# One transformer layer on one core: the first chunk's front of the last stage placed beside attention's last group

## The reference, cut to what matters

```python
x   = L0_attn_x                                   # (4, 1024, 128), 16 heads of 8
S   = Q @ K^T / sqrt(8), causal;  attn = softmax(S);  O = attn @ V
x1  = layernorm(x + O @ W_o.T + b_o)
sim = (x1 @ Wq) against keys                      # 2 x 4 heads x 64 keys per token
sx, sy = top 8 of each half;  scores = top 8 of sx[i] + sy[j]      # per head
w   = silu(x1 . down_embed[idx]) * softmax(scores)
y   = silu(x1 @ Wg + bg) * (x1 @ Wu + bu) @ Wd + bd + sum_k w_k * up_embed[idx_k]
out = layernorm(x1 + y)
```

## Time and profile before

| | us |
|---|---|
| median of 3 runs (840.32 to 843.26) | 842.15 |
| the profiled execution | 842.8 |
| its span on the core | 841.1 |
| TensorE busy | 731.9 (87%) |
| Vector busy | 683.3 (81%) |
| ScalarE busy | 567.9 (68%) |
| GpSimd busy | 423.4 (50%) |
| granted TensorE clock, mean | 0.941 of full |

### The profile page before, as it was taken

How to read it: one execution, slowest core, us unless ns; L and a number is a source line. 1 busy time by engine, 2 the same in 40 slices (tenths; PEclk the granted TensorE clock), 3 DMA queues, 4 the chain that set the end, 5 groups by cost and what they waited for, 6 DMA issues and landing times. The chain is left out here.

```text
span 841.1 us, 17303 instructions
## 1 busy us (share of the span) xinstructions
PE 731.9 (87%) x4345; PEld 328.1 (39%) x4345; DVE 683.3 (81%) x2289; ACT 567.9 (68%) x926; POOL 423.4 (50%) x468
## 2 busy tenths in 40 slices
PE   6768999999999999999999998677888798888755
PEld 4422333333333333333333332333556456555345
DVE  5979998998998989989989971066888888888883
ACT  4710466766676766667757678368879788897771
POOL 8880121122112211322132212368999999999984
PEclk9965799999999999999999999698999999999997
DMA  7984435533653454436433331201010101100000
GB/s 195 278 219 93 98 94 120 126 86 82 130 125 74 91 131 115 87 80 140 115 81 85 84 84 35 76 4 50 1 38 1 39 0 39 39 1 13 14 1 26
DMA packets 58954, 67.05 MB, mean 80 GB/s; under 512 B 15488, under 2 KB 33536, under 8 KB 58880
## 3 DMA queue, kind: packets, MB, share of 16 engines
q1 hardware_dynamic: 53120, 62.35, 31.2%
q10 hardware_dynamic: 5184, 2.36, 1.0%
q0 software_dynamic: 576, 1.57, 0.6%
HBM read 46.73 MB, written 19.53 MB: 79 GB/s over the span
## 5 line engine op out<-in xcount | busy, mean ns | idle before, releaser
L699 ACT ACTIVATE probs<-ps 128x384 f32<-128x384 f32 (+2 forms) x384 | 291.5, 809 | 175.1 <-PE ps L753 172.9
L670 POOL TENSOR_SCALAR_AFFINE_SELECT probs<-probs 128x256 f32<-128x256 f32 x256 | 102.8, 406 | 363.3 <-ACT probs L699 360.7
L721 PE MATMUL ps<-Kx,Qx 128*128 128x512 bf16 (+3 forms) x768 | 232.5, 348 | 20.4 <-DVE mx L813 11.0
L809 DVE CUSTOM_DVE_ANT_0 junk<-ps,tri 128x256 bf16<-128x256 f32 (+3 forms) x512 | 228.7, 488 | 21.2 <-PE ps L721 18.0
L753 PE MATMUL ps<-Qa,Ka 128*128 128x512 bf16 (+3 forms) x768 | 180.3, 329 | 3.3 <-ACT probs L699 2.9
L813 DVE TENSOR_REDUCE mx<-ps 128x1 f32<-128x512 f32 x256 | 162.1, 681 | 17.6 <-issue 11.7
L739 PE MATMUL ps<-probs,Vg 128*9 128x512 f32 (+3 forms) x1536 | 153.3, 488 | 0.3 <-POOL probs L670 0.3
L721 PEld LDWEIGHTS ps<-Kx,Qx 128*128 128x128 bf16 x768 | 69.6, 98 | 210.9 <-DVE mx L809 85.2
L968 POOL TENSOR_TENSOR S<-sim 128x1024 f32<-128x1024 f32 x64 | 120.6, 1907 | 11.7 <-DVE A L1220 6.5
L1220 DVE SCALAR_TENSOR_TENSOR A<-S,T,ps 128x511 f32<-128x511 f32 x128 | 90.1, 741 | 11.2 <-ACT ps L1042 10.2
L1042 ACT ACTIVATE ps<-S,nb 128x512 f32<-128x512 f32 x128 | 82.9, 679 | 11.9 <-DVE A L1220 11.7
(11 more groups left out here) (115 smaller groups left out, 857.7 us busy)
## 6 DMA issues: line engine op xcount, KB each, us to landing
Qx<-q_scr SPq DMA_DIRECT2D x48, 192.0 KB
Kx<-k_scr SPq DMA_DIRECT2D x48, 192.0 KB
Qa<-q_scr SPq DMA_DIRECT2D x48, 192.0 KB
Ka<-k_scr SPq DMA_DIRECT2D x48, 192.0 KB
o_scr<-Os SPq DMA_DIRECT2D x32, 256.0 KB, 2.1
q_scr<-qs SPq DMA_DIRECT2D x34, 128.0 KB, 3.4
k_scr<-qs SPq DMA_DIRECT2D x18, 128.0 KB, 3.9
xin<-in_L_attn_x_dram ACTq DMA_DIRECT2D x8, 256.0 KB, 4.3
```

Of the source, the lines that this page charges most:

```text
L670: pool.affine_select(out=diag, in_=diag, compare_op=ALU.is_ge, fill=0.0, base=0, pattern=[[0, 2], [1, P]], channel_multiplier=-1).then_inc ...
L699: act.activation(probs[:, k % 2, hh, 0:width], ps[:, bank:bank + 2, :].rearrange("p a c -> p (a c)")[:, 0:width], ACT.Exp, scale=SM_SCALE) ...
L721: pe.matmul(ps[:, X_BANK + f % X_SLOTS, 0:c1 - c0], Qx[:, u, hh, P * i:P * (i + 1)], Kx[:, u, hh, c0:c1], start=True, stop=True).then_inc( ...
L809: dve.tensor_tensor_reduce(out=junk[:, f % 4, 0:w], in0=src, in1=tri[:, CHUNK - w:CHUNK], scale=1.0, scalar=-BIG, op0=ALU.add, op1=ALU.max ...
```

## The change

The front of chunk 0 leaves the last stage (`EARLY`, which takes its words out of all four orders, and so out of the ring) and is written into attention's block:

- SyncE loads the softmax sums after group 13 instead of after group 14, that is, ahead of group 14's first wait, and stores the reciprocals and loads chunks 0 and 1 (`first_rows`) between group 14's first store and `m_rows(15)`.
- Vector inverts the sums inside group 14, ahead of step f = 24 (`RCP_AT`).
- Between groups 14 and 15 GpSimd does `weigh` and `rstd`, TensorE starts group 15 with `early_sum`, ScalarE does the squares. Inside group 15 TensorE does the turn ahead of score step 5 and the sims ahead of steps 8, 10, 12 and 14. Vector, free in that group, does norm, both x1T copies, the sim copies, tops, candidates and thresholds.
- GpSimd does the S sums of t = 0 and 1 ahead of its ninth mask tile of group 15 and those of t = 2 and 3 after its last.
- The buffers of the front overlay `Qx`/`Kx`, `qs` and `vaug`. The weights and biases keep their places in time.

The diff, cut to its core:

```diff
+RCP_AT = 24
...
+EARLY = {(name, 0) for name in ("weigh", "sum", "sp", "rstd", "norm", "turn", "xt", "sim", "cs", "s", "top", "cand", "t")}
+TURN_AT, SIM_AT, S_AT = 5, (8, 10, 12, 14), (8, 8, 16, 16)
...
-            if 0 <= c + ahead < CHUNKS:
+            if 0 <= c + ahead < CHUNKS and (name, c + ahead) not in EARLY:
...
+                    def first_rows():
+                        sp.wait_ge(rcp_made, 1)
+                        sp.dma_start(r_scr[0:BATCH - 1].rearrange("b p t -> p b t"),
+                                     dn[:, 0:BATCH - 1, :]).then_inc(rcp_stored, 16)
+                        sp.wait_ge(rcp_stored, 16)
+                        for c in range(2):
+                            load_att(sp, c)
+                    def group(n, u, ahead, between=None):
                         sp.wait_ge(s_ready, SPG * n + ONE)
                         load_parts(sp, Qa[:, 1 - u], Ka[:, 1 - u], bass.ds(n + 1, 1), sop_loaded[1 - u])
                         store_o(n, 0)
+                        if between is not None:
+                            between()
...
-                    group(GROUPS - 2, 0, False)
-
                     for half in range(2):
                         sp.wait_ge(o_stored[half], 16 * HG * (BATCH - 1) + ONE)
                     for b in range(BATCH - 1):
                         load_dens(sp, b)
+                    group(GROUPS - 2, 0, False, first_rows)
                     store_o(GROUPS - 1, 0)
-
-                    sp.wait_ge(rcp_made, 1)
-                    sp.dma_start(r_scr[0:BATCH - 1].rearrange("b p t -> p b t"),
-                                 dn[:, 0:BATCH - 1, :]).then_inc(rcp_stored, 16)
-                    sp.wait_ge(rcp_stored, 16)
-                    for c in range(2):
-                        load_att(sp, c)
...
+                    def early_sums(t):
+                        pool.wait_ge(sim0_copied, t + 1)
+                        for g in range(2):
+                            heads = sim[:, t, :].rearrange("p (w h k) -> p w h k", w=2, h=RH)[:, :, 2 * g:2 * g + 2, :]
+                            pool.tensor_tensor(S[:, t, 2 * g:2 * g + 2, :].rearrange("p h (x y) -> p h x y", x=XIN),
+                                               heads[:, 0, :, 0:XIN].unsqueeze(3).broadcast_to([P, 2, XIN, NK]),
+                                               heads[:, 1].unsqueeze(2).broadcast_to([P, 2, XIN, NK]),
+                                               ALU.add).then_inc(s_made, 1)
+                    def group(n, last=False):
                         for r, k in enumerate(DIAG_UNITS):
                             step = UNITS[k][1][1][3]
                             for hh in range(GH):
+                                for t in range(TPC):
+                                    if last and S_AT[t] == GH * r + hh:
+                                        early_sums(t)
                                 wait_alone(pool, exp_done, SPG * n + GH * k + hh + 1 + FREE, pads_made)
                                 diag = probs[:, k % 2, hh, 0:2 * step].rearrange("p (a c) -> p a c", a=2)[:, :, 0:P]
                                 pool.affine_select(out=diag, in_=diag, compare_op=ALU.is_ge, fill=0.0, base=0,
                                                    pattern=[[0, 2], [1, P]], channel_multiplier=-1).then_inc(masked, 1)
-                    with pool.Fori(0, GROUPS) as n:
+                    with pool.Fori(0, GROUPS - 1) as n:
                         group(n)
+                    pool.wait_ge(att_loaded[0], 32)
+                    pool.wait_ge(v_staged, 2 + GROUPS)
+                    pool.tensor_tensor(attnT[:, 0, :], attO[:, 0, :], rcpB[:, 0, :], ALU.mult).then_inc(attnT_ready, 1)
+                    pool.wait_ge(var_ready, 1)
+                    pool.tensor_tensor(rstd[:, 0, 0, :], veps[:, 0, 0, :], mhalf[:], ALU.pow).then_inc(rstd_ready, 1)
+                    group(GROUPS - 1, True)
+                    for t in range(TPC):
+                        if S_AT[t] >= MPG:
+                            early_sums(t)
...
+                    act.activation(eps_col[:], mhalf[:, 0:1], ACT.Copy, bias=EPS, scale=0.0).then_inc(consts_made, 1)
+                    act.wait_ge(y_ready, 1)
+                    for t in range(TPC):
+                        if t >= 2:
+                            act.wait_ge(sq_done, t - 1)
+                        act.activation(squares[:, t % 2, :], ps[:, X_BANK, P * t:P * (t + 1)], ACT.Square,
+                                       scale=float(D) ** -0.5, accum_out=ss[:, 0, 0, t:t + 1]).then_inc(sq_done, 1)
+                    act.wait_ge(sq_done, TPC)
+                    act.wait_ge(consts_made, 6)
+                    act.activation(veps[:, 0, 0, :], ss[:, 0, 0, :], ACT.Identity, bias=eps_col[:, 0:1]).then_inc(var_ready, 1)
+                    group(GROUPS - 1)
...
+                    def early_sum():
+                        pe.wait_ge(mx_read, CPG * GROUPS)
+                        pe.wait_ge(attnT_ready, 1)
+                        pe.wait_ge(xb_made, CHUNKS)
+                        for t in range(TPC):
+                            dst = ps[:, X_BANK, P * t:P * (t + 1)]
+                            pe.matmul(dst, attnT[:, 0, P * t:P * (t + 1)], WoC[:], start=True, stop=False)
+                            mm = pe.matmul(dst, xbT[:, 0, P * t:P * (t + 1)], center[:], start=False, stop=True)
+                        mm.then_inc(y_ready, 1)
+                    def early_turn():
+                        pe.wait_ge(x1_ready, 1)
+                        for t in range(TPC):
+                            mm = pe.transpose(ps[:, X_BANK, P * t:P * (t + 1)], x1[:, t, :], ident[:])
+                        mm.then_inc(x1T_ready, 1)
+                    def early_sims(t):
+                        pe.wait_ge(x1T_copied, 2)
+                        if t >= 2:
+                            pe.wait_ge(sim0_copied, t - 1)
+                        pe.matmul(ps[:, X_BANK + 1 + t % 2, :], x1T[:, 0, P * t:P * (t + 1)],
+                                  Wsim[:].rearrange("p a b -> p (a b)"), start=True, stop=True).then_inc(sim0_ready, 1)
                     def group(n, u, turn, last):
                         e = f = r = 0
+                        if last == 2:
+                            early_sum()
                         for step in GROUP_ORDER:
+                            if step == "s" and last == 2 and e == TURN_AT:
+                                early_turn()
+                            if step == "s" and last == 2 and e in SIM_AT:
+                                early_sims(SIM_AT.index(e))
...
+                            if f == RCP_AT and last == 1:
+                                dve.wait_ge(dn_loaded, 16 * HG * (BATCH - 1))
+                                dve.reciprocal(dn[:, 0:BATCH - 1, :], dn[:, 0:BATCH - 1, :]).then_inc(rcp_made, 1)
...
-                    dve.wait_ge(dn_loaded, 16 * HG * (BATCH - 1))
-                    dve.reciprocal(dn[:, 0:BATCH - 1, :], dn[:, 0:BATCH - 1, :]).then_inc(rcp_made, 1)
+                    dve.wait_ge(rstd_ready, 1)
+                    dve.tensor_tensor(x1[:], ps[:, X_BANK, :].rearrange("p (t d) -> p t d", t=TPC),
+                                      rstd[:, 0, 0, :].unsqueeze(2).broadcast_to([P, TPC, D]), ALU.mult).then_inc(x1_ready, 1)
+                    dve.wait_ge(x1T_ready, 1)
+                    dve.tensor_copy(x1T[:, 0, :], ps[:, X_BANK, :]).then_inc(x1T_copied, 1)
+                    dve.tensor_scalar(x1bT[:, 0, :], ps[:, X_BANK, :], bd_col[:, 0:1], None, ALU.add).then_inc(x1T_copied, 1)
+                    for t in range(TPC):
+                        dve.wait_ge(sim0_ready, t + 1)
+                        dve.tensor_copy(sim[:, t, :], ps[:, X_BANK + 1 + t % 2, :]).then_inc(sim0_copied, 1)
+                        dve.wait_ge(sim0_copied, t + 1)
+                        for g in range(2 * RH):
+                            last = dve.max(V[:, g // RH, RH * t + g % RH, :], sim[:, t, NK * g:NK * (g + 1)])
+                        last.then_inc(top_made, 1)
+                    for p in range(2):
+                        these = slice(2 * RH * p, 2 * RH * (p + 1))
+                        dve.wait_ge(top_made, 2 * p + 2)
+                        dve.tensor_tensor(cand[:, these, 0:2 * KPH].rearrange("p j (a b) -> p j a b", a=2),
+                                          V[:, 0, these, 0:2].unsqueeze(3).broadcast_to([P, 2 * RH, 2, KPH]),
+                                          V[:, 1, these, :].unsqueeze(2).broadcast_to([P, 2 * RH, 2, KPH]), ALU.add)
+                        dve.tensor_tensor(cand[:, these, 2 * KPH:].rearrange("p j (a b) -> p j a b", b=2),
+                                          V[:, 0, these, 2:].unsqueeze(3).broadcast_to([P, 2 * RH, KPH - 2, 2]),
+                                          V[:, 1, these, 0:2].unsqueeze(2).broadcast_to([P, 2 * RH, KPH - 2, 2]),
+                                          ALU.add).then_inc(cand_made, 1)
```

(16 more changed lines are left out.)

49 lines of the change are left out of this document (26 added, 23 removed).

## The result

The changed kernel took 845.86 us (median of 8 runs, 843.84 to 847.82) where the one before took 842.28 beside it (8 runs): ratio 1.0048, interval 1.0031 to 1.0064. That is 3.6 us slower; forecast were +3.5 and 845.7. The profiled execution has a span of 846.1 us, 5.0 above the 841.1 of before.

What follows compares the result with a forecast made beforehand. GpSimd's queue was taken to pace the last stage, with a 35.6 us pipeline fill to move into idle time. 7.4 + 4.35 + 2.15 + 5.3 - 15.7 = +3.5 us gave 845.7 us, range 838.8 to 850.5 (8 in 10).

Steps and rivals of the forecast that it cites:

- Part 2 (A): Group 14: Vector waits 3.9 us for early-loaded sums before inverting, stalling ScalarE 6.35 plus 1.0 for clock; cost 7.4 us.
- The paragraph on SyncE's queue: Groups 14 to 15: chunk 0's rows there by 512 us, row maxima by about 515, covered by 5 us.
- Part 3 (B): Hand-over from group 14 to 15: weigh, sum, squares and products delay the next exp; cost 4.35 us, clock taken as kept.
- rival 3: Hand-over: TensorE loses its clock (+2.0 us) and its products run at half clock (+1), 848.7 us; chance 0.20.
- Part 4 (C): Inside group 15: the added turn and four sims on TensorE cost 2.15 us; GpSimd's first four sums fit without waits.
- Part 5 (D): Attention's tail: four GpSimd sums behind its last mask delay the barrier from 532.73 to 538.1 us; cost 5.3 us.
- Part 1: Last stage: chunk 0's first exps come closer to the barrier that opens the stage; gain 15.7 us.
- ScalarE begins at T0 with the table load: Last stage: ScalarE's table load starts right at the barrier, with 19.9 us from there to chunk 0's first exps.
- From e0 on nothing changes: Last stage: behind chunk 0's first exps the engines run as before, GpSimd's queue full to the end; no change.
- Rival 1: Group 14: the wait for the sums costs nothing, only 1.5 to 2 us lost, total 840 us; chance 0.12.
- rival 2: Last stage: warm start, first exps 17 us behind the barrier, gain 18.5 us, total 842.9 us; chance 0.18.
- rival 4: Group 15: chunk 0's rows or m_rows(15) land late behind Qa and Ka, whole core waits, 850 us or more; chance 0.07.

Runs made afterwards that it cites:

- e1: Kernel before with only the softmax-sum loads ahead of group 14 and the inversion at step 24, front left in the last stage: 851.57 us, ratio 1.0107.
- the repetition: The changed kernel measured again, nothing altered: 848.0 us, ratio 1.0056 to the kernel before.
- e4: Changed kernel with chunk 0's S sums of token tiles 2 and 3 put back into the last stage: 843.49 us, ratio 1.0003 to the kernel before.
- e2: Changed kernel with the 12 softmax-sum loads issued earlier, in group 13 behind m_rows(14): 843.49 us, ratio 1.0014 to the kernel before.
- b2: b1 with the start flag on only the first of the four split-sum matmuls, so everything is computed: 832.43 us, ratio 0.9872 to the kernel before.
- e3: Changed kernel with only the inversion moved from step 24 to step 30, behind group 15's row maxima: 848.99 us, ratio 1.0078 to the kernel before.
- b4: Changed kernel with the edits of e2, e3 and e4 together, and chunk 1's rows loaded behind m_rows(15): 835.4 us, ratio 0.9906 to the kernel before.
- e6: Changed kernel with two unused 128x512 filler matmuls ahead of TensorE's wait for attnT in the hand-over: 847.33 us, ratio 1.007 to the kernel before.
- b3: b4 with e6's two filler matmuls ahead of the hand-over wait: 833.7 us, ratio 0.9887 to the kernel before.
- e5: Changed kernel with the hand-over sum's four x-only matmul pairs ahead of TensorE's wait for attnT, start flag on each: 846.87 us, ratio 1.0058 to the kernel before.
- b1: b4 with e5's split sum, start flag on each of the four, so x parts are missing: 831.92 us, ratio 0.9876 to the kernel before.

## Why the prediction was right, and where it wasn't

The direction was right, and four of the five terms came within 0.8 us of their forecast. That the time came out within 0.2 us is luck: errors of up to 2 us, of both signs, nearly cancel.

**Part 2 (A), forecast 7.4, measured 7.78** (7.89 alone in e1, 6.99 in the repetition). Vector's wait was put at 3.9 and was 3.72, ScalarE's at 6.35 and was 5.93; the clock's share was put at 1.0, and the exps behind show another idle time of 1.71 in e1 and the changed kernel, 1.11 in e4, 0.82 in the repetition. The sums landed 1.48 us behind the end of the last load's issue, where the row had given 1.65. The mechanism holds step by step. The paragraph on SyncE's queue does not: it took the hop of the reciprocals at 2.1 us from the earlier trace rows, and it was 7.0, with six loads of Qa and Ka issued in the 4 us ahead of the store. e2 and b2, with those loads issued 5 us and more ahead of it, have 2.8 and 2.1. The 12 small loads don't make it: in both kernels, before and changed, the last of them had been issued 4.1 to 4.2 us ahead of the store. The rows of chunk 0 were due by 512; the issue of the last of them ended at 510.54, and by e3, where the same load was done 3.3 us behind its issue, they were there by about 513.9. `weigh` began at 516.09, so its cover was about 2 us, and there only because A itself had pushed the masks back. `m_rows(15)` was put at 507; its store stands at 511.87 and its last load was issued by 517.1, 5.5 us ahead of group 15's first score (522.63). The Trainium skill (DMA: Bandwidth & Descriptors, Anatomy of one DMA) gives a fixed cost of about 2.0 us, in a section on DMAs that GpSimd issues; the 2.1 of this SyncE store in b2 is near it, the 7.0 is not. That the loads ahead make the difference is shown; whether they held the queue or the transfer itself is not.

**Part 3 (B), forecast 4.35, measured 6.08** (b, 7.70 against 1.62; 5.90 in the repetition, 5.9 to 6.1 in e2, e4 and b4 too), inside the bound of 6.5 given for a lost clock. This is the step that failed: "I take it as kept, since group 14 ended fully busy" was wrong, and the first half of rival 3 was right. The term was mis-sized by 1.7, and the filler gives back 1.6 of it in e6 and 1.5 in b3: with the clock kept, b is 6.07 in both, so B is 4.45, as good as the 4.35 forecast. The fall came up to 1.0 us behind the idle time in the changed kernel and e2 and within it in the repetition, e4 and b4, each time with 2.39 us of idling.

**Part 4 (C), forecast 2.15, measured 2.73**, inside the bounds; 21.79 to 21.81 in all kernels with the front there, so it is the steadiest term. GpSimd's first four sums fit in as worked out.

**Part 5 (D), forecast 5.3, measured 5.09**; e4 takes all of it away. It was priced right as a cost, and not seen as a choice: the sums of two token tiles gain nothing by standing there. Vector's candidates of 128x96, priced at 0.99 us each, took 0.26 us at 540.4 and 541.6, between GpSimd's two blocks of sums and beside neither. So the port pair that the prediction weighed had no case here.

**Part 1, forecast 15.7, measured 14.89 to e0.** The step "ScalarE begins at T0 with the table load" is wrong: the load stands at 557.08, 2.3 us behind the barrier, since it began only when TensorE's first matmuls had made what the activation behind it reads (in e4 as well). From there to e0 it took 18.3 us, not 19.9, so the two errors nearly meet. "From e0 on nothing changes" is wrong too, by -2.02 (-2.88 in the repetition). The waits view of GpSimd from 575 us on (waited for: us in total, times, longest):

```profile
POOL D L1085 <- DVE rows L1300: 3.1, 5, 0.7
POOL QK L1075 <- DVE A L1325: 3.1, 2, 1.5
```

The same view of the kernel before, from its e0 on:

```profile
POOL D L978 <- DVE T L1195: 1.5, 3, 0.6
```

Before, the sums waited 6.5 us for Vector's masks; here it is 3.1, while the waits of `D` for the top values rise from 1.5 to 3.1. Over all kernels the waits of the sums and the distance from e0 to the end go together: 3.1 us in the five with 269.9 to 270.8 (both runs of the changed kernel, e2, e3, e5), 4.6 in b1 with 271.1, 5.1 in e6, b3 and b2 with 271.6 to 272.2, 6.5 to 6.6 in before, e1, e4 and b4 with 272.3 to 272.8. Where two sums are put back into the last stage's beginning (e4 and the b kernels) the waits are longer, but that alone does not settle it: e6, which keeps all sums early, has 5.1. What decides them was not tried.

**The sum.** Errors of +0.4, +1.7, +0.6, -0.2, +0.8 and -2.0 (rounded) make the +1.2 by which the ledger (+4.73) exceeds the forecast (+3.5); the medians (+3.6) lie between, within what one profile differs from the next. Rival 1 fell (e1), rival 2 fell (20.59 behind the barrier, not 17), rival 3 held for the sum and its products, but at 1.6 us and not the 3 that it was given, rival 4 was near and came out in e3.

## What to carry to other kernels

A wait put into an in-order queue costs whatever is queued behind it on every engine that follows; look for the last place where its result still comes in time, and then follow the result's own transfers, because a stall can hide a second lateness that shows only once the first is mended. A step moved beside other work must be moved in pieces: those that lie on the new path's end (here the last sums) go back, and those that need nothing of the late operand go ahead of the wait, where they also kept TensorE's clock. A change that seems to be a small loss may be a large gain with a few misplaced steps: here +3.6 us as it stood, -10.3 mended.

## What the runs showed of the hardware

- The store of the reciprocals (192 KB) had landed 2.1 us behind its issue in the kernel before and the b kernels, 2.3 in e1, 2.8 in e2, and 6.5 to 7.0 us behind it in the six kernels in which six loads of Qa and Ka (192 KB each) had been issued in the 4 us ahead of it (changed, its repetition, e3 to e6), though the issue itself took 0.39 us.
- TensorE's clock fell to the lower level at an idle time of only 2.39 us, behind some 12 us or more of nearly gapless work (changed, its repetition, e2, e4, b4); with 0.57 (e6, b3) and 1.40 us (e5, b1, b2) it stayed at 1.00. Idle times of 2.1 us went both ways: one in e2 (496.32 to 498.41) was followed by the lower level, one in the changed kernel (581.95 to 584.04) was not.
- The table load on ScalarE did not run ahead into an idle time: in the changed kernel ScalarE idled 8.19 us in front of it (2.13 in e4), until TensorE had made what the next activation reads, and only then spent 1.28 us on the load. Whether the load could stand ahead of that wait was not tried.
- The start flag of a matmul acts on more than the region it writes. With four open sums in one PSUM bank and the flag on each (e5, b1), x parts already summed were lost; with the flag on the first alone all four were whole (b2). Which token tiles lose theirs stands in no trace. The Trainium skill (PSUM — Partial Sum Buffer, The four PSUM rules) says that the flag clears the written-marks of the whole bank (for the partitions written), after which a matmul without it overwrites; the runs agree, and by that rule only the last tile would keep its part.
